# Norm statistics on ScalarE, image additions on TensorE and state buffers four chunks wide in a four-stage convolution and state-space kernel

## What is computed

```python
x = x + conv3x3(_gn(x))      # stage 1: ReLU of the image times a mask around its centre of mass, then 3x3 conv
x = x + updown(_gn(x))       # stage 2: upsample by 2 (12 taps), leaky ReLU and clip, downsample by 2
x = x + ssm_pyramid(_gn(x))  # stage 3: 1x1 convs, 3 sizes of image, state-space scans forwards and backwards
x = x + updown(_gn(x))       # stage 4: as stage 2, other filters
```

```python
def step(h, inp):
    da, dbx, c = inp
    h = h * da + dbx
    return (h, jnp.einsum('bdn,bn->bd', h, c))
```

## Time and profile before

| | |
|---|---|
| time, median of 3 runs | 6978.4 us (6974.67 to 6983.81) |
| the profiled execution, its own time | 6980.12 us |
| its span, first to last instruction | 6978.3 us |
| DVE busy | 6424.6 us, 92% |
| PE busy | 5898.9 us, 85% |
| ACT busy | 3611.4 us, 52% |
| POOL busy | 157.5 us, 2% |
| DMA | 546.08 MB, mean 78 GB/s |
| granted TensorE clock, mean | 0.889 of full speed |

### The profile page before, as it was taken

One profiled execution on the slowest core, in us unless ns is written; L12 is line 12 of the kernel. 1 busy time (PEld: TensorE's weight loads), 2 busy tenths in 40 slices (PEclk: granted clock), 3 DMA queues, 4 the chain that ended last, 5 costly groups with the idle time before them and its releaser, 6 DMA issues.

```text
span 6978.3 us, 92012 instructions
## 1 busy us (share of the span) xinstructions
PE 5898.9 (85%) x32140; PEld 3815.7 (55%) x32140; DVE 6424.6 (92%) x8557; ACT 3611.4 (52%) x6466; POOL 157.5 (2%) x69
## 2 busy tenths in 40 slices
PE   5788888988888988889988889888889888899875
PEld 3455555655555555556555556555556555565543
DVE  2899999999999999999999999999999999999996
ACT  1455455555555555555554555554555555555553
POOL 0000000000000000000000000000000000000000
PEclk9898898989899988889888889888889888899877
DMA  1323323323323323323233233233233233232231
GB/s 44 87 63 86 90 69 85 91 53 96 83 70 90 79 65 90 86 69 90 68 81 90 72 82 91 57 92 84 72 86 85 59 90 89 68 92 70 74 91 50
DMA packets 323883, 546.08 MB, mean 78 GB/s; under 512 B 104710, under 2 KB 173646, under 8 KB 323290
## 3 DMA queue, kind: packets, MB, share of 16 engines
q1 hardware_dynamic: 323420, 540.18, 30.7%
HBM read 269.28 MB, written 33.12 MB: 43 GB/s over the span
## 4 chain that ended last, share of the span: by engine, by line
PE 26%; DVE 25%; issue 12%; SPq 5%; DMA 4%; ACT 3%; DVEq 0%; ACTq 0%
PE ps L624 8%; DVE hb L1196 7%; PE ps L674 5%; PE ps L655 4%; DVE hb L1215 4%; DVE hb L1180 4%; SPq L570 3%; DMA dx_t<-vc 2%; DVE ys L1130 2%; DMA delta_t<-vd 2%; PE ps L767 2%; DVE lines L1058 2%; PE ps L637 1%; PE ps L783 1%; PE ps L762 1%
## 5 line engine op out<-in xcount | busy, mean ns | idle before, releaser
L1196 DVE TENSOR_TENSOR_SCAN hb<-da,hb 128x784 f32<-128x784 f32 (+2 forms) x1344 | 2355.9, 1779 | 14.2 <-ACT da L952 12.3
L624 PE MATMUL ps<-pad,conv_w 128*128 128x392 f32 x4608 | 1659.7, 507 | 15.5 <-ACT pad L844 15.5
L1215 DVE TENSOR_TENSOR hb<-hb,c_t 128x784 f32<-128x784 f32 x1344 | 1265.5, 974 | 0.0
L624 PEld LDWEIGHTS ps<-pad,conv_w 128*128 128x128 f32 x4608 | 862.4, 194 | 695.6 <-issue 155.1
L674 PEld LDWEIGHTS ps<-down_k,ys 121*128 121x128 f32 x9216 | 1126.3, 198 | 111.4 <-issue 48.8
L674 PE MATMUL ps<-down_k,ys 121*128 121x121 f32 (+1 forms) x9216 | 1145.6, 281 | 34.4 <-DVE ys L1130 24.6
L655 PE MATMUL ps<-xt,up_k 123*121 123x256 f32 (+2 forms) x4096 | 1115.1, 417 | 7.8 <-ACT xt L852 7.7
L952 ACT ACTIVATE da<-delta_t,a_neg 128x784 f32<-128x784 f32 x1024 | 926.2, 940 | 314.0 <-DVE hb L1196 313.1
L860 ACT ACTIVATE ys<-ps 121x512 f32<-121x512 f32 x1152 | 674.5, 595 | 712.2 <-PE ps L655 445.6
L1180 DVE TENSOR_TENSOR hb<-dx_t,b_t 128x784 f32<-128x784 f32 x1024 | 956.0, 965 | 43.5 <-PE ps L767 43.2
L655 PEld LDWEIGHTS ps<-xt,up_k 123*121 123x121 f32 x4096 | 630.6, 184 | 390.9 <-ACT ys L860 206.7
(11 more groups left out here) (118 smaller groups left out, 5428.7 us busy)
## 6 DMA issues: line engine op xcount, KB each, us to landing
delta_t<-vd SPq DMA_DIRECT2D x256, 392.0 KB, 6.6
b_t<-scr SPq DMA_DIRECT2D x256, 392.0 KB, 4.3
dx_t<-vc SPq DMA_DIRECT2D x256, 392.0 KB, 6.6
c_t<-scr SPq DMA_DIRECT2D x256, 392.0 KB, 4.4
xr<-in_x SPq DMA_DIRECT2D x32, 784.0 KB, 4.4
out<-xr SPq DMA_DIRECT2D x32, 784.0 KB, 8.7
delta_t<-vd SPq DMA_DIRECT2D x128, 98.0 KB, 2.4
dx_t<-vc SPq DMA_DIRECT2D x128, 98.0 KB, 2.4
```

Source lines behind the costliest of these rows:

```text
L624: mm = nc.tensor.matmul(ps[:, half, 0:HALF], conv_w[:, c, tap, m * P:(m + 1) * P], pad[:, c, r0:r0 + HH // 2, tap % 3:tap % 3 + WW], start ...
L1196: nc.vector.tensor_tensor_scan(h, a, b, 0.0, ALU.mult, ALU.add).then_inc(scan_done, 1)
L1215: nc.vector.tensor_tensor(v, v, c, ALU.mult).then_inc(hc_done, 1)
```

## The change

It does six things, and gives all four tables a new order.

1. Group statistics move from DVE to ACT. For each chunk ACT runs a pass with Identity and `accum_out` (the sum) and a pass with Square of the image minus the mean and `accum_out` (the variance), and writes mean and bias by itself. Where a step on ACT writes the image anyway (`ca`, `x3`) the sum comes with that. `bn_stats`, `bn_aggr`, `g1` and `g3` are gone from DVE, `group_dev` from PE.
2. Old image plus result: PE adds the image by a matmul with the identity into the same PSUM group (4 for conv, 4 for `bo`); `ca` and `x3` become ACT copies with bias.
3. The centre of mass: four DVE `scalar_tensor_tensor` with `accum_out` in place of the two reductions and the small sums behind them.
4. State buffers hold four chunks: `hb` is 2 buffers of 4 by 785 in place of 6 of 1, `da` is one buffer filled in halves in place of 3. Per sample there are 10 `db`, 22 `sc` (1570 or 1576 long) and 12 `hc` (3136 long).
5. Images: one buffer `xa` for stages 1 and 2, one buffer `xb` for the end of stage 3 and stage 4. Between them a sample goes to HBM (`spill`) and comes back (`back`). A load now waits for the spill and the norm of the sample just before it.
6. Stage 4 of a sample runs one round later than before (offsets 3 and 4 in place of 2 and 3).

The diff, cut to its core (the tables, counters and renamed waits are left out):

```diff
-        xr = [sb(f"xr{i}", [P, NC, HW]) for i in range(3)]
+        xa = sb("xa", [P, NC, HW])
+        xb = sb("xb", [P, NC, HW])
...
-        delta_t = [sb(f"delta_t{j}", [P, HW]) for j in range(4)]
-        dx_t = [sb(f"dx_t{j}", [P, HW]) for j in range(4)]
+        delta_t = sb("delta_t", [P, 4, HW])
+        dx_t = sb("dx_t", [P, 4, HW])
...
-        NA, NB = 3, 6
-        RW = 16 * (LEN[2] + 1)
-        da = [sb(f"da{i}", [P, RW]) for i in range(NA)]
-        hb = [sb(f"hb{i}", [P, RW]) for i in range(NB)]
+        RW = 16 * (LEN[1] + 1)
+        da = sb("da", [P, RW])
+        hb = [sb(f"hb{i}", [P, RW]) for i in range(2)]
...
-        bcr = sb("bcr", [P, HW])
...
-        st = [sb(f"st{i}", [P, NC, 2, 6]) for i in range(4)]
-        mv = [sb(f"mv{i}", [P, NC, 2]) for i in range(4)]
-        gmd = [sb(f"gmd{i}", [P, 4]) for i in range(4)]
-        dev2 = [sb(f"dev2{i}", [P, NC]) for i in range(4)]
+        gsum = [sb(f"gsum{i}", [P, 2, NC]) for i in range(4)]
+        gsq = [sb(f"gsq{i}", [P, NC]) for i in range(4)]
+        nmean = [sb(f"nmean{i}", [P, NC]) for i in range(4)]
...
+        bcr = msk
...
+        xs = nc.dram_tensor("xs", [N_SAMPLES, P, NC, HW], F32, kind="Internal").ap()
...
                 def load(s):
-                    if s >= 3:
-                        sp.wait_ge(y_stored, 16 * (s - 2))
-                    sp.dma_start(xr[s % 3][:, :, :], sample(t["x"], s)).then_inc(x_loaded[s % 3], 16)
-
-                def store(s):
+                    if s:
+                        sp.wait_ge(x_spilled, 16 * s)
+                        sp.wait_ge(gn_act[B_GN], normed(B_GN, s - 1, 1))
+                    sp.dma_start(xa[:, :, :], sample(t["x"], s)).then_inc(x_loaded, 16)
...
+                def spill(s):
+                    sp.wait_ge(layer_added, 2 * chunk_pass(FIRST, s, 1) + 2)
+                    sp.dma_start(xs[s], xa[:, :, :]).then_inc(x_spilled, 16)
+
+                def back(s):
+                    sp.wait_ge(x_spilled, 16 * (s + 1))
                     if s:
                         sp.wait_ge(y_stored, 16 * s)
+                    sp.dma_start(xb[:, :, :], xs[s]).then_inc(x_back, 16)
...
+                def store(s):
                     sp.wait_ge(layer_added, 2 * chunk_pass(LAST, s, 1) + 2)
-                    sp.dma_start(sample(t["out"], s), xr[s % 3][:, :, :]).then_inc(y_stored, 16)
+                    sp.dma_start(sample(t["out"], s), xb[:, :, :]).then_inc(y_stored, 16)
...
                 def gm1(s, k):
                     out = take_ring("gm1", s, k)
-                    pe.wait_ge(gn_vec[k], 10 * s + 6)
-                    nc.tensor.matmul(out[:, 0:2], group_mean[:, :], mv[k][:, :, 0], start=True, stop=True)
-                    nc.tensor.matmul(out[:, 2:4], group_dev[:, :], mv[k][:, :, 0], start=True, stop=True).then_inc(gn_mm[k], 1)
+                    if k == FIRST_GN:
+                        pe.wait_ge(conv_added, 4 * (s + 1))
+                    elif k == LAST_GN:
+                        pe.wait_ge(x3_done, 2 * (s + 1))
+                    else:
+                        pe.wait_ge(gn_act[k], gn_at(k, s, 0))
+                    n = 2 if k == FIRST_GN else 1
+                    for half in range(n):
+                        mm = nc.tensor.matmul(out[:, 0:2], group_mean[:, :], gsum[k][:, half, :], start=(half == 0), stop=(half == n - 1))
+                    mm.then_inc(gn_mm[k], 1)
...
+                    if n == 0:
+
+                        nc.tensor.matmul(ps[:, half, 0:HALF], ident[:, :], xa[:, m, half * HALF:(half + 1) * HALF], start=True, stop=False)
...
-                                              start=(i == 0), stop=(i == NC * TAPS - 1))
+                                              start=False, stop=(i == NC * TAPS - 1))
...
                     out = take("bo", s, m)
                     pe.wait_ge(gated, s + 1)
+                    pe.wait_ge(x_back, 16 * (s + 1))
                     for half in range(2):
+                        nc.tensor.matmul(out[:, half, 0:HALF], ident[:, :], xb[:, m, half * HALF:(half + 1) * HALF], start=True, stop=False)
                         mm = nc.tensor.matmul(out[:, half, 0:HALF], out_w[:, m * P:(m + 1) * P],
-                                              y1[:, half * HALF:(half + 1) * HALF], start=True, stop=True)
+                                              y1[:, half * HALF:(half + 1) * HALF], start=False, stop=True)
...
+                def gp(s, k, c):
+                    if c == 0 and k == CONV_GN:
+                        act.wait_ge(x_loaded, 16 * (s + 1))
+                    if k == B_GN:
+                        act.wait_ge(layer_added, 2 * chunk_pass(FIRST, s, c) + 2)
+                    spare_free(s, k, c)
+                    nc.scalar.activation(spare(k, c), image(k, c), ACT.Identity, accum_out=gsum[k][:, 0, c:c + 1]).then_inc(gn_act[k], 1)
...
+                def gq(s, k):
+                    act.wait_ge(gn_mm[k], 2 * s + 1)
+                    nc.scalar.activation(nmean[k][:, :], ring("gm1", s, k)[:, 0:2], ACT.Copy, scale=-1.0).then_inc(gn_act[k], 1)
...
+                def gv(s, k, c):
+                    act.wait_ge(gn_act[k], gn_at(k, s, 1))
...
+                    nc.scalar.activation(spare(k, c), image(k, c), ACT.Square, bias=nmean[k][:, c:c + 1],
+                                         accum_out=gsq[k][:, c:c + 1]).then_inc(gn_act[k], 1)
...
+                    act.wait_ge(gn_act[k], gn_at(k, s, 5))
+                    for c in range(NC):
+                        nc.scalar.activation(nbias[k][:, c:c + 1], nmean[k][:, c:c + 1], ACT.Copy, scale=rstd[k][:, c:c + 1]).then_inc(gn_act[k], 1)
...
-                                             scale=rstd[k][:, c:c + 1]).then_inc(gn_act[k], 1)
+                        nc.scalar.activation(inner(c), image(k, c), ACT.Identity, bias=bias, scale=scale,
+                                             accum_out=s0[:, c:c + 1]).then_inc(gn_act[k], 1)
...
                     n = LEN[lev]
-                    v = seg(buf, q)
-                    nc.scalar.copy(v[:, :, n], zero[:, 0:(16, 4)[q]]).then_inc(pad_done, 1)
-                    for m in range((16, 4)[q]):
-                        a = m if q == 0 else 4 * i + m
-                        ins = nc.scalar.activation(v[:, m, 0:n], delta_t[j][:, (m % 4) * n:(m % 4 + 1) * n], ACT.Exp, scale=a_neg[:, w, a:a + 1])
+                    part = p[0] if p else 0
+
+                    if u >= 3:
+                        act.wait_ge(scan_done, last_scan(s, u - 1) - 1 + part)
+                    elif u:
+                        act.wait_ge(scan_done, last_scan(s, u - 1))
+                    elif s:
+                        act.wait_ge(scan_done, last_scan(s - 1, N_UNIT - 1))
...
+                    else:
+                        for j in (2 * part, 2 * part + 1):
+                            a = 4 * ((u - 2) % 4) + j
+                            act.wait_ge(d_in[j], 16 * tile_full(s, q, j))
+                            ins = nc.scalar.activation(v[:, j, 0:n], delta_t[:, j, :], ACT.Exp, scale=a_neg[:, w, a:a + 1])
...
+                def mr(s, a, c):
+
...
+                        dve.wait_ge(mask_vec, 20 * s + 2 * c + a)
+                    dve.wait_ge(gn_act[CONV_GN], normed(CONV_GN, s, c))
+                    by = ramp[:, :].unsqueeze(2 - a).broadcast_to([P, HH, WW])
+                    nc.vector.scalar_tensor_tensor(out=img(msk[:, :]), in0=inner(c), scalar=1.0, in1=by, op0=ALU.mult, op1=ALU.mult,
+                                                   accum_out=s1[:, a, c:c + 1]).then_inc(mask_vec, 1)
...
-                    v = pad[:, :, 1:HH + 1, 1:WW + 1]
-                    nc.vector.tensor_reduce(lines[:, n, :, :], v if n == 0 else v.rearrange("p c h w -> p c w h"), AX, ALU.add).then_inc(mask_vec, 1)
...
-                def ca(s, g):
-                    m, half = divmod(g, 2)
-                    dve.wait_ge(conv_sum, 4 * s + g + 1)
-                    v = xr[s % 3][:, m, half * HALF:(half + 1) * HALF]
-                    nc.vector.scalar_tensor_tensor(out=v, in0=ps[:, half, 0:HALF], scalar=conv_b[:, m:m + 1], in1=v,
-                                                   op0=ALU.add, op1=ALU.add).then_inc(conv_added, 1)
...
+                def db(s, u):
+                    q = UNITS[u]
+                    lev = BRANCH[q][0]
+                    n = LEN[lev]
+                    i = USE_AT[(u, 1 if q != 2 else 0)]
+                    if N_USE * s + i >= 2:
+                        dve.wait_ge(red_done, N_USE * s + i - 1)
+                    v = seg(hb[i % 2], lev)
+                    if u <= 3:
+                        nc.vector.memset(v[:, :, n], 0.0).then_inc(pad_done, 1)
...
                     else:
-                        nc.vector.tensor_tensor(buf[:, 0:HW], dx_t[j][:, :], b_t[u % 2][:, :], ALU.mult).then_inc(db_done, 1)
...
+                        nc.vector.tensor_tensor(v[:, :, 0:n], dx_t[:, :, :], b_t[u % 2][:, :].unsqueeze(1).broadcast_to([P, 4, n]),
```

(14 more changed lines are left out.)

513 lines of the change are left out of this document (221 added, 292 removed).

## The result

The changed kernel takes 6594.7 us (median of 4, 6592.3 to 6600.7) against 6981.1 before (median of 4): ratio 0.9449, 95% interval 0.9432 to 0.9465. That is faster, 386 us, inside the range, and 202 us above the forecast of 6393. The profiled execution has a span of 6590.5 us.

A forecast was written before the change was run, and what follows sets the result against it. DVE was taken to bound the kernel: 178.2 us of work plus 15 idle make a 193 us round, with PE and the image-buffer loop about as long. 32 rounds plus 215 us of start and end gave 6393 us, range 6160 to 6680.

The forecast's parts named there:

- the second rival: PE's 189.3 us set the round if its clock stays at 0.89: round 200.5 us, time 6631; chance 0.15.
- The terms of DVE: DVE work a round: statistics -10.8, image additions -4.0, mask -1.5, merging -5.4, from 199.9 to 178.2 us.
- (c): Mask on DVE: four scalar_tensor_tensor with accumulator replace two reductions and small sums, -1.5 us a round.
- (d): Merging on DVE: 77 fewer hc, db and scan instructions, 0.07 us each, -5.4 us a round.
- The loop of `xa`: Single image buffer's cycle of load, norms, conv, stage 2 and spill: 178 us a round, about as long as DVE's work.
- today's idle time of DVE is 11.8 us. I take 15, a quarter more: DVE idle time a round, added to 178.2 us of work because DVE, PE and the image-buffer cycle are similarly long.
- 203.9 plus some 11 for a pipeline one round deeper = 215: Start and end of the span, outside the 32 rounds: 203.9 us before, 215 forecast.
- the third rival: The image buffer's cycle sets the round at 216 us because spill, load and norms find queues busy: 7127 us; chance 0.06.
- Merging returns its full fixed part: Each merged DVE instruction saves 0.14 us, DVE 172, round 185, and other cycles hide: 6137 us; chance 0.17.
- The loop of `xa` decides: The single image buffer's cycle is slower, 216 us a round, and sets the time: 7127 us; chance 0.06.
- PE becomes the bound: With the clock still at 0.89, PE's 189.3 us plus idle share give 200.5 a round, 6631 us; chance 0.15.

The follow-up runs named there:

- the unmerged run: Changed kernel with the products with B and C over four tiles as four instructions again, 54 more on DVE a round: 6652.0 us, ratio 0.9533 to the kernel before.
- fillers: Changed kernel plus nine or ten matmuls a round on PE whose results nobody reads, placed where PE waits for norms: 6480.2 us, ratio 0.9291 to the kernel before.

## Why the prediction was right, and by how much it was off

| step of the prediction | forecast | measured |
|---|---|---|
| DVE work, us a round | 178.2 (172 to 184) | 180.1 |
| ACT work | 131.8 | 128.5 |
| PE work | 168 to 189 | 181.9 |
| DVE idle | 15 | 17.5 |
| round | 193 | 197.6 |
| start and end | 215 | 268.1 |

- **Where the result lies.** The range held it, but not through my own mechanism: the 6230 to 6550 that I gave 0.58 leaves 6594.7 out, and the stretch that holds it, 6550 to 6680, was priced for the second rival, whose 6631 is nearer (36 us) than my 6393 (202 us). 588 us of gain were forecast, 386 came. To that extent the hit is luck.
- **The terms of DVE** nearly held, their sum 1.9 us too low. (c): 100 mask forms of 971 ns, with 83 ns for each accumulator read, make 4.2 us a round. (d): 0.060 us per merged instruction against my 0.07, so the 77 give 4.6 and not 5.4 if the scans do as the products do; that is 0.8 of the 1.9, and the rest was not traced. The wide product takes 3.41 us, under the 3.6 that would have refuted it. The Trainium skill's figure (VectorE: DVE Perf Modes, the section on the TRN2 errata) gives an estimate of (3136 + 151) / 0.96 = 3424 ns, and the trace agrees with 3415; but the saving of the whole fixed part per instruction less, which the rival built on, is refuted by the unmerged run. The Trainium skill's rule against (c) (Vector Engine (DVE) Microarchitecture Reference, Points that are easy to get wrong) does not hold for this form: two fp32 sources and an accumulator run at 971 ns, not halved.
- **ACT** came out 3.3 lower, although the accumulator reads are 187 ns and the biases 287, above my 0.1 and 0.203. I had added durations of single instructions, and busy time counts neighbours that overlap once; that this is all of it was not tried.
- **The loop of `xa`** does not decide, but it has less room than the 15 us between 178 and 193. In the round shown the load is issued at 3111.7, as the norm ahead of stage 3 ends, lands 4.3 us later, and is read at 3119.5: 3.5 us of room. The doubled load, of 4.4 us or more, cost 1.3. How long the loop is by itself no run shows.
- **The step that failed first** is "today's idle time of DVE is 11.8 us. I take 15, a quarter more". The size was near, the mechanism not. I let DVE set the round and added what coupling costs. The runs show that no engine sets it alone: 4.9 us less DVE work gave 19 us, 5.3 us less PE work none, both together 102. For 140 us of a round PE and DVE are full at once, and 56 us run in series at a lowered clock. Of the 4.6 us that the round is longer than forecast, 1.9 are DVE work and 2.5 idle time (193 was rounded from 193.2). With the clock held up by fillers the round is 194.0, near the forecast, but for another reason than it gave.
- **The mis-sized term** is "203.9 plus some 11 for a pipeline one round deeper = 215". With 32 x 4.57 = 146 us the round is most of the 202, and this term is 53. The 203.9 came from one round of 211.70 us; by the mean of 25 rounds, 211.51, the kernel before has 210.0, which is 6 of the 53. The start and end grew by 58 us in place of 11. The places are in the start times of stage 3's last product, before and after:

```profile
L1248 DVE SCALAR_TENSOR_TENSOR y<-y,bias_sum,sz x32: 997/1004/1036, 432.9 to 6920.8; 128x784 f32<-128x784 f32 x32
```

```profile
L1257 DVE SCALAR_TENSOR_TENSOR y<-y,bias_sum,sz x32: 1022/1028/1035, 434.4 to 6508.4; 128x784 f32<-128x784 f32 x32
```

The first comes as late as before although a round is 13.9 us shorter: +15. After the last, the kernel before needs 57.5 us and this one 82.1: +25. The longest wait of PE in those 82 us accounts for 9.1 of them:

```profile
PE ps L801 <- DMA xb<-xs: 9.1, 1, 9.1
```

The last sample's image can come back into the only `xb` once the sample before is stored. My reading is that two stages 4 that could stand close therefore run one behind the other. Some 19 more lie in the last two rounds: 356.4 us before, 67 less than two full ones, and 347.6 now, 48 less. No run tried these places, so their cause stays open.

- **The signs named.** DVE 5785 us busy (5700 named), but 88% of the span, not 92; wide products 3.4 (3.3); mean clock 0.935 (above 0.92); the round 197.6, not near 193. DVE's wait for `pad` is 2.7 us, far from the 20 of the third rival.
- **The rivals.** "Merging returns its full fixed part" is refuted. "The loop of `xa` decides" is refuted. "PE becomes the bound" gave 6631 and a range that holds the result, and it had the right hint in the clock, but its mechanism (PE's busy time sets the round) is refuted by the run without identity matmuls and with the z product on DVE.

## What to carry to other kernels

When two engines are each about 90% busy, ask in which stretch each is full: where both are, work taken from one alone may bring next to nothing (19 us and none here, 102 from both), and may cost time by what then collides. Before weighing a reordering, list every buffer that ties unlike steps together (here the mask and the copies of B and C). Where TensorE pauses for small serial steps and the work behind the pause is on the path, idle matmuls into a buffer that it already holds are worth a trial.
